# A Mamba and FFN layer on one core: dt products in pairs of row halves, the normalisation in four items, later stores, new order lists

## What is computed

```
xi, z = split(x @ W_in.T)                     # 512 + 512 channels
u  = silu(causal_conv4(xi) + conv_b)
dbl = u @ W_xproj.T                           # 16 (dt) + 16 (B) + 16 (C) columns
dt = softplus(dbl[:, :16] @ W_dt.T + b_dt)
h_t = h_(t-1) * exp(dt_t * A) + (dt_t * u_t) * B_t     # 512 channels x 16 states
y_t = sum_s h_t * C_t + u_t * D_skip
x1 = layernorm(x + (y * silu(z)) @ W_out.T)
out = layernorm(x1 + (silu(x1 @ wg.T) * (x1 @ wu.T)) @ wd.T)   # hidden width 768, int weights / 127
```

## Time and profile before

| | us |
|---|---|
| median of 3 runs | 1813.12 (1812.05 to 1816.79) |
| the profiled execution, its time | 1811.88 |
| its span, first to last instruction | 1810.2 |

### The profile page before, as it was taken

How to read it: one execution, slowest core, us unless ns; L and a number is a source line. 1 busy time by engine, 2 the same in 40 slices (tenths; PEclk the granted TensorE clock), 3 DMA queues, 4 the chain that set the end, 5 groups by cost and what they waited for, 6 DMA issues and landing times.

```text
span 1810.2 us, 40427 instructions
## 1 busy us (share of the span) xinstructions
PE 1738.4 (96%) x15678; PEld 1214.1 (67%) x15678; DVE 1708.0 (94%) x2003; ACT 1714.3 (95%) x2907; POOL 1496.8 (83%) x852
## 2 busy tenths in 40 slices
...
GB/s 209 1 119 1 23 98 15 118 1 114 19 15 118 14 118 1 59 74 15 117 10 123 1 15 118 15 118 1 90 43 15 118 12 120 1 54 67 1 25 24
DMA packets 171487, 100.57 MB, mean 56 GB/s; under 512 B 139408, under 2 KB 157584, under 8 KB 163232
## 3 DMA queue, kind: packets, MB, share of 16 engines
...
...
## 4 chain that ended last, share of the span: by engine, by line
PE 44%; ACT 28%; DVE 14%; issue 9%; POOL 4%; DMA 1%; SPq 0%; ACTq 0%; POOLq 0%; DVEq 0%
PE ring L1172 16%; PE tp L1151 13%; ACT decay L702 9%; ACT hT L709 8%; DVE h L913 7%; PE yb L1165 7%; PE ring L1264 4%; DVE acc L934 4%; POOL drive L568 3%; PE ring L1209 2%; ACT L739 2%; ACT acc L718 1%; ACT sz L739 1%; PE ring L1230 1%; ACT u L735 1%
## 5 line engine op out<-in xcount | busy, mean ns | idle before, releaser
L568 POOL TENSOR_TENSOR drive<-dtu,b_all 128x1024 f32<-128x1024 f32 x511 | 1217.1, 2417 | 9.7 <-DVE h L913 7.4
L702 ACT ACTIVATE decay<-dt,a_neg 128x512 f32<-128x512 f32 x1024 | 706.8, 718 | 9.5 <-DVE h L913 8.7
L1151 PEld LDWEIGHTS tp<-ident,h 128*128 128x128 f32 x4096 | 463.3, 141 | 251.4 <-issue 122.4
L913 DVE TENSOR_TENSOR_SCAN h<-decay,h,drive 128x512 f32<-128x512 f32 x512 | 620.8, 1268 | 8.7 <-ACT decay L702 4.5
L913 DVE TENSOR_TENSOR_SCAN h<-decay,drive 128x512 f32<-128x512 f32 x512 | 592.6, 1209 | 26.0 <-ACT decay L702 23.4
L709 ACT ACTIVATE hT<-tp 128x512 f32<-128x512 f32 x1024 | 596.8, 619 | 20.5 <-PE tp L1151 19.6
L1151 PE MATMUL tp<-ident,h 128*128 128x128 f32 x4096 | 564.2, 277 | 45.8 <-ACT hT L709 32.8
L1165 PE MATMUL yb<-hT,diag_c 128*32 128x128 f32 x8192 | 275.5, 277 | 6.5 <-ACT yt L730 5.3
L1165 PEld LDWEIGHTS yb<-hT,diag_c 128*32 128x32 f32 x8192 | 210.6, 110 | 82.0 <-issue 47.9
L1172 PE MATMUL ring<-xt,w_in 128*128 128x512 f32 x512 | 245.1, 602 | 2.4 <-ACT acc L750 2.4
L934 DVE SCALAR_TENSOR_TENSOR acc<-xi,cw,acc 128x512 f32<-128x512 f32 x189 | 160.0, 867 | 14.1 <-ACT xi L720 10.2
...
## 6 DMA issues: line engine op xcount, KB each, us to landing
b_all<-bc_scratch SPq DMA_DIRECT2D x63, 1024.0 KB, 6.9
xt<-in_xT SPq DMA_DIRECT2D x16, 512.0 KB, 4.4
res<-in_x SPq DMA_DIRECT2D x16, 512.0 KB, 5.8
out<-res SPq DMA_DIRECT2D x15, 512.0 KB, 2.9
c_col<-bc_scratch SPq DMA_DIRECT2D x256, 2.0 KB, 2.4
...
b_all<-bc_scratch SPq DMA_DIRECT2D x2, 512.0 KB, 4.6
...
```

The costliest lines, as they stand in the source:

```text
L568: tt(drive[:, j % 4, :, :], src, b_all[:, n:n + 2, :], ALU.mult).then_inc(g_dr, 1)
L702: act(decay[decay_slot(k.parity, i)][:, :], dt[:, cb, :], ACT.Exp, scale=a_neg[:, cb, n:n + 1]).then_inc(a_da, 1)
L913: nc.vector.tensor_tensor_scan(h[:, h_slot(k.parity, q), at:at + T, i % 4], decay[decay_slot(k.parity, i)][:, :], drive[:, (i // 2) % 4, i ...
L1151: last = nc.tensor.transpose(tp[g % 2][:, b * P:(b + 1) * P], h[:, h_slot(k.parity, q), t0:t0 + TS, :].rearrange("p t s -> p (t s)"), iden ...
```

## The change

**dt products.** w_dt gets a second copy of its 16 rows in rows 64 to 79, and from chunk 1 on a DMA on SP copies dbl's rows 0 to 15 into rows 64 to 79. In first and steady chunks dt 0 and 1, and dt 2 and 3, are issued as a pair, the first through rows 0 to 63, the second through rows 64 to 127, after a wait for both banks.
**Normalisation.** norm is four list items of one instruction each, with the same wait in each.
**Stores.** store(k-2) stands at the end of SP's chunk.
**Lists.** All lists are new. The core of the diff, with the steady lists in the places that the prediction speaks of:

```diff
 PE_SIDE = {
-    (0, 1): [("sum", 14)], (0, 3): [("z", 0)], (1, 1): [("sum", 15), ("z", 1), ("turn", 3)],
...
-    (5, 2): [("x1T", 0), ("sum", 3), ("x1T", 1)], (6, 0): [("gate", 0)], (6, 1): [("gate", 1)],
-    (6, 2): [("sum", 4)], (6, 3): [("up", 0), ("gate", 2), ("up", 1)], (7, 1): [("sum", 5), ("xproj", 0)],
-    (7, 3): [("gate", 3)], (8, 1): [("sum", 6), ("turn", 0)], (8, 3): [("gate", 4)], (9, 1): [("dt", 0)],
-    (9, 2): [("sum", 7)], (9, 3): [("gate", 5)], (10, 1): [("up", 2)], (10, 3): [("sum", 8)],
-    (11, 1): [("up", 3)], (11, 3): [("up", 4), ("sum", 9), ("sum", 10)], (12, 0): [("turn", 1)],
-    (12, 1): [("up", 5)], (12, 3): [("dt", 1), ("sum", 11)], (13, 1): [("down", 0), ("turn", 2)],
-    (13, 3): [("down", 1)], (14, 1): [("sum", 12)], (14, 3): [("dt", 2)], (15, 1): [("dt", 3)],
-    (15, 3): [("sum", 13)],
+    (0, 1): [("sum", 14)], (0, 3): [("xi", 0), ("sum", 15)], (1, 1): [("z", 0), ("turn", 3)],
...
+    (4, 1): [("x1T", 0), ("x1T", 1), ("sum", 2)], (4, 2): [("gate", 0)], (4, 3): [("gate", 1)],
+    (5, 0): [("up", 0), ("up", 1)], (5, 2): [("gate", 2)], (5, 3): [("sum", 3)], (6, 1): [("xproj", 0)],
+    (6, 3): [("sum", 4)], (7, 0): [("gate", 3)], (7, 2): [("gate", 4)], (7, 3): [("sum", 5)],
+    (8, 1): [("sum", 6)], (8, 3): [("up", 2)], (9, 1): [("turn", 0)], (9, 3): [("sum", 7)],
+    (10, 1): [("dt", 0), ("dt", 1)], (10, 2): [("sum", 8)], (10, 3): [("up", 3)], (11, 1): [("gate", 5)],
+    (11, 3): [("sum", 9)], (12, 0): [("sum", 10)], (12, 2): [("turn", 1)], (12, 3): [("up", 4)],
+    (13, 1): [("sum", 11)], (13, 3): [("up", 5), ("sum", 12), ("turn", 2)], (14, 1): [("down", 0)],
+    (14, 3): [("dt", 2), ("dt", 3)], (15, 1): [("down", 1)], (15, 3): [("sum", 13)],
 }
 ACT_SIDE = {
...
-    (3, 1): [("log", 1)], (3, 2): [("hT", 8), ("hT", 9)], (3, 3): [("xi", 1)], (4, 1): [("sz", 0), ("sz", 1)],
...
-    (6, 0): [("hT", 19), ("hT", 20), ("u", 0), ("hT", 21), ("u", 1), ("y", 0), ("tanh", 0), ("tanh", 1), ("u", 2), ("u", 3), ("hT", 22)],
-    (6, 3): [("tanh", 2), ("hT", 23), ("norm", 1)], (7, 0): [("hT", 24)], (7, 1): [("hT", 25)],
...
-    (11, 0): [("hT", 41)], (11, 1): [("hT", 42), ("hT", 43)], (11, 3): [("sz", 2)],
...
-    (13, 2): [("hT", 48)], (13, 3): [("sz", 3), ("hT", 49), ("log", 0)], (14, 2): [("hT", 50), ("hT", 51)],
...
+    (2, 1): [("hT", 5), ("z", 1)], (2, 2): [("hT", 6), ("z", 2)], (2, 3): [("hT", 7)], (3, 2): [("log", 1)],
+    (4, 0): [("sz", 0)], (4, 1): [("xi", 1), ("hT", 8), ("hT", 9)], (4, 3): [("hT", 10), ("xi", 2)],
+    (5, 0): [("hT", 11), ("xi", 3), ("hT", 12), ("z", 3), ("x1T", 0), ("x1T", 1), ("hT", 13), ("u", 0), ("hT", 14), ("u", 1), ("sz", 1), ("tanh", 0), ("u", 2), ("tanh", 1), ("hT", 15), ("u", 3)],
...
+    (10, 0): [("hT", 35), ("y", 1)], (10, 1): [("hT", 36)], (10, 2): [("hT", 37), ("bias", 0)],
+    (10, 3): [("hT", 38)], (11, 0): [("hT", 39), ("bias", 1)],
...
+    (13, 2): [("y", 2), ("hT", 50), ("hT", 51)], (14, 0): [("sz", 2), ("sz", 3), ("log", 0), ("hT", 52)],
+    (14, 1): [("hT", 53)], (14, 2): [("hT", 54), ("hT", 55), ("bias", 2)], (14, 3): [("hT", 56)],
+    (15, 1): [("hT", 57), ("norm", 1)], (15, 3): [("hT", 58), ("hT", 59), ("bias", 3)],
 }
 DVE_SIDE = {
-    (2, 1): [("skip", 3), ("clamp", 1)], (3, 3): [("conv", 0, 0), ("r1", 0)], (4, 2): [("r1", 1)],
-    (5, 3): [("max", 1), ("norm", 0), ("conv", 0, 1), ("conv", 1, 0), ("conv", 1, 1), ("conv", 2, 0), ("conv", 2, 1), ("conv", 3, 0), ("conv", 3, 1)],
-    (6, 0): [("gs", 0), ("gs", 1)], (6, 2): [("hid", 0)], (7, 0): [("gs", 2)], (7, 1): [("hid", 1)],
-    (8, 2): [("gs", 3), ("skip", 0)], (9, 2): [("gs", 4)], (10, 3): [("hid", 2), ("gs", 5)],
-    (11, 3): [("hid", 3), ("hid", 4)], (12, 1): [("skip", 1)], (12, 2): [("hid", 5)],
-    (14, 0): [("clamp", 0), ("r2", 0), ("skip", 2)], (14, 1): [("max", 0)], (15, 0): [("r2", 1)],
+    (1, 1): [("clamp", 1)], (1, 3): [("skip", 3)], (3, 2): [("r1", 0)], (4, 0): [("r1", 1)],
+    (4, 3): [("max", 1), ("conv", 0, 0), ("norm", 0, 0), ("norm", 0, 1), ("norm", 0, 2), ("norm", 0, 3), ("conv", 0, 1), ("conv", 1, 0), ("conv", 1, 1), ("conv", 2, 0), ("conv", 2, 1), ("conv", 3, 0), ("conv", 3, 1)],
+    (5, 0): [("gs", 0)], (5, 1): [("gs", 1)], (5, 2): [("hid", 0)], (6, 1): [("hid", 1)], (7, 1): [("gs", 2)],
+    (8, 1): [("gs", 3)], (8, 3): [("gs", 4)], (10, 0): [("skip", 0), ("hid", 2)], (11, 1): [("hid", 3)],
+    (12, 0): [("gs", 5)], (13, 1): [("skip", 1)], (13, 3): [("hid", 4), ("hid", 5), ("clamp", 0)],
+    (14, 0): [("skip", 2)], (14, 2): [("max", 0), ("r2", 0)], (15, 3): [("r2", 1)],
 }
...
 ACT_END = [
...
+    ("hT", 55), ("sz", 2), ("hT", 56), ("hT", 57), ("sz", 3), ("hT", 58), ("hT", 59), ("end_hT", 60), ("end_hT", 61),
...
 POOL_LAST = {
...
-    (4, 1): [("std", 0), ("diag", 3)], (7, 0): [("dtu", 1)], (11, 1): [("gate", 0)], (12, 1): [("gate", 1)],
-    (15, 0): [("gate", 2)],
...
+    (7, 0): [("dtu", 1)], (10, 1): [("gate", 0)],
 }
 POOL_END = [
-    ("end_std", 1),
+    ("gate", 1), ("gate", 2), ("end_std", 1),
 ]
...
             (w_dt[0:R, :], W_dtT),
+            (w_dt[P // 2:P // 2 + R, :], W_dtT),
...
             def spread_bc(k, with_b=False):
                 wait(eng, a_dbl, k.count(2, 2))
+                if k.index > 0:
+                    eng.dma_start(dbl[P // 2:P // 2 + R, :], dbl[0:R, :]).then_inc(st_two, 16)
                 eng.dma_start(bc_dram, dbl[R:R + 2 * N, :]).then_inc(st_bc, 16)
...
             def chunk(k, tail, head, more, late=True):
                 if tail:
                     load_res(k + -1)
-                if late:
-                    store(k + -2)
                 if head:
                     spread_bc(k + 1)
...
                         load_b(g)
+                if late:
+                    store(k + -2)
...
-            def normalise(k):
+            def normalise(k, blocks):
 
                 wait(eng, g_n[0], k.count(4, 4))
-                for tb in range(TB):
+                for tb in blocks:
...
-                if tail:
+                if what == "norm" and tail:
+                    normalise(k + -1, part)
+                elif tail:
                     rest_of_layer(k + -1, what, i)
...
+            def dt_pair(k, cb):
+
+                if cb == 0:
+                    eng.wait_ge(st_two, 16 * k.index)
+                room(place["dt", cb, k.index])
+                room(place["dt", cb + 1, k.index])
+                for i in range(2):
+                    rows = slice(i * P // 2, (i + 1) * P // 2)
+                    product(bank(k, "dt", cb + i)[:, :], [(w_dt[rows, (cb + i) * P:(cb + i + 1) * P], dbl[rows, :])], p_dt)
...
+                elif what == "dt" and kind != "last":
+                    if of[0] % 2 == 0:
+                        dt_pair(k + 1, of[0])
```

More of the change, by code:

```diff
@@ L96 @@
+    (15, 1): [("gate", 2), ("dtu", 0), ("diag", 0)],
 }
 PE_FIRST = {
-    (0, 3): [("xi", 0)], (1, 1): [("z", 0)], (1, 3): [("xi", 1)], (2, 2): [("z", 1)], (2, 3): [("xi", 2)],
-    (3, 0): [("sum", 0)], (3, 1): [("sum", 1)], (3, 3): [("sum", 2)], (4, 2): [("z", 2)], (5, 0): [("z", 3)],
-    (5, 2): [("sum", 3), ("xi", 3)], (7, 0): [("sum", 4)], (7, 1): [("sum", 5), ("xproj", 0)],
-    (8, 3): [("turn", 0), ("dt", 0), ("sum", 6)], (9, 1): [("sum", 7)], (9, 3): [("dt", 1)],
-    (10, 3): [("sum", 8)], (11, 1): [("sum", 9)], (11, 2): [("dt", 2)], (12, 0): [("turn", 1)],
@@ L105 @@
+    (12, 3): [("dt", 0), ("dt", 1), ("sum", 10), ("sum", 11), ("turn", 2)], (14, 0): [("sum", 12)],
+    (14, 3): [("dt", 2), ("dt", 3)], (15, 3): [("sum", 13)],
 }
 ACT_FIRST = {
[16 rows of a table removed]
[15 rows of a table added]
 }
 DVE_FIRST = {
-    (0, -1): [("clamp", 1)], (2, 2): [("max", 1)], (3, 2): [("conv", 0, 0)],
-    (7, 0): [("conv", 0, 1), ("conv", 1, 0), ("conv", 1, 1), ("conv", 2, 0), ("conv", 2, 1), ("conv", 3, 0), ("conv", 3, 1)],
-    (10, 0): [("skip", 0)], (12, 3): [("skip", 1)], (13, 0): [("clamp", 0)], (13, 3): [("max", 0)],
@@ L128 @@
-    (14, 2): [("skip", 2)],
+    (0, -1): [("clamp", 1)], (1, 0): [("conv", 0, 0)], (5, 3): [("conv", 0, 1), ("max", 1), ("conv", 1, 0)],
+    (6, 1): [("conv", 1, 1)], (9, 1): [("conv", 2, 0), ("conv", 2, 1), ("conv", 3, 0), ("conv", 3, 1)],
+    (9, 3): [("skip", 0)], (11, 0): [("skip", 1)], (13, 1): [("clamp", 0)], (13, 2): [("skip", 2)],
+    (14, 0): [("max", 0)],
 }
 POOL_FIRST = {
-    (3, 0): [("first_diag", 0), ("first_diag", 1)], (3, 1): [("first_diag", 2)], (5, 1): [("first_diag", 3)],
@@ L137 @@
-    (2, 0): [("turn", 3)], (2, 1): [("sum", 0)], (2, 3): [("out", 0)], (3, 1): [("out", 1)],
-    (3, 3): [("sum", 1)], (4, 0): [("z", 3)], (4, 3): [("sum", 2), ("sum", 3)],
-    (5, 0): [("x1T", 0), ("x1T", 1)], (5, 2): [("gate", 0)], (5, 3): [("gate", 1)], (6, 0): [("gate", 2)],
-    (6, 2): [("up", 0)], (6, 3): [("up", 1), ("turn", 0), ("sum", 4), ("sum", 5)], (7, 1): [("up", 2)],
-    (7, 3): [("gate", 3)], (8, 1): [("sum", 6)], (8, 3): [("gate", 4)], (9, 0): [("up", 3)],
```

(25 more changed lines are left out.)

49 lines of the change are left out of this document (25 added, 24 removed), and 82 rows, old and new, of tables (ACT_FIRST, ACT_LAST, ACT_SIDE).

## The result

The changed kernel takes 1874.18 us (median of 4 runs, 1871.68 to 1874.88); the kernel before took 1812.59 beside it. The ratio is 1.0336, 95% interval [1.0318, 1.0354]: **61.6 us slower**, where 18.6 faster was forecast, far outside the range.

What follows compares the result with a forecast made beforehand. Even chunks were taken as bound by ACT and PE, odd by DVE. Seven pairs at 2.3 us (-16), with +0.6 -2 -3 +1.7, took 1811.9 to 1793; plus 1.2 for the median, 1794.5, range 1785 to 1810.

Steps and rivals of the forecast that it cites:

- The change takes nothing off DVE: DVE's work stays, so two chunks cannot fall below 212.95 us from 216.05; at most 3.1 us per pair.
- nine short ones, 0.67 each: DVE's gs, hid, skip and clamp instructions from skip 0 to r2 0, counted at 6 us of 28.
- 6 us of cover: Slack from DVE having 37 us to skip 0 where PE has 31 to turn 0; meant to absorb the bank waits.
- Bank waits costed at nothing: Each dt pair on PE waits for two free ring banks; this was put at nothing on DVE's path.
- rival B: PE stands at pair two for a scan, max 0 and r2 0's add, 2.2 us per chunk: 1831; chance 0.08.
- PE -0.70 per chunk: Pairs save PE 1.14 us per chunk, extra detours return 0.44; two chunks fall from 213.78 to 212.4.
- D: Row halves do not run beside each other on PE, adding 0.58 and 0.43 us per chunk: 1824; chance 0.04.
- Odd chunks by DVE: DVE, busy 106.96 of 108.13 us, was read as what bounds odd chunks.
- even chunks are bound by ACT and PE: Of an even chunk's 107.92 us ACT is busy 107.53 and PE 106.49, so these were read as its bound.
- The burst: DVE's convolutions move behind scan 19 with one more tap, about 11 us with max 1 and norm.
- What would show it: Signs set beforehand; wrong if odd chunks exceed 108.5 us, PE stands before w_dt for DVE, or w_dt steps stay 0.43.
- case C: PE stands about 0.7 us per chunk for pair two's second bank, leaving time unchanged at 1811; chance 0.10.

Runs made afterwards that it cites:

- e6: The changed kernel with the clamp in a one-port form that also reduces into a spare column: 1813.88 us, 1.0016 of the kernel before.
- e7: The changed kernel with r2 0 ahead of max 0 on DVE in the steady chunks, old clamp kept: 1870.04 us, 1.0326 of the kernel before.
- e11: The changed kernel with single dt products instead of pairs and the one-port clamp: 1822.27 us, 1.0059 of the kernel before.
- e12: e6 with five tile detours joined in PE's steady list: 1873.58 us, 1.0343 of the kernel before.
- e14: e6 with two detours joined in PE's steady list, sum 8 behind dt 0 and 1, sum 10 beside sum 9: 1818.58 us.
- e8: The kernel before with sz 2 moved beside sz 3 on ACT in steady chunks, meant to save two table loads per chunk: 1818.2 us, 1.0041.
- e4: The kernel before with only the store moved to the end of SP's chunk: 1809.7 us, 0.9998.
- e1: The changed kernel with heads on POOL moved from (5, 0) to (6, 1) in the steady list: 1903.37 us, 1.0518 of the kernel before.

## Why the prediction was wrong

- **"The change takes nothing off DVE", floor 212.95 per two chunks: the step that failed.** It is true of the work and false of the time: the wait for GpSimd inside the clamp was put at nothing, without a reason. I carried the clamp at 0.67 us through a change of all lists; it took 4.1, 14 times, and 2.7, 6 times, which is 14 x 3.4 + 6 x 2.05 = 60 us. e6 gets 59 us back. Of these 42 are DVE's time in the clamps, whose new form is no longer blocked but slower by itself; the rest is what followed from them. The "nine short ones, 0.67 each" of the count from skip 0 to r2 0 hold the same clamp: 3.4 of the 6 us of cover went there. The cue stood in the trace before, in the group of the taps and in the timeline shown above:

```profile
L934 DVE SCALAR_TENSOR_TENSOR acc<-xi,cw,acc 128x512 f32<-128x512 f32 x189 | 160.0, 867 | 14.1 <-ACT xi L720 10.2
```

A mean of 867 ns where most taps take 0.75 us, and a clamp of 0.97 at 554.23 beside a drive of 2.81 instead of 2.38. A group whose mean lies above its shortest instruction has a second price, set by what runs beside it, and no list of counts shows it.
- **Bank waits costed at nothing, and rival B.** The wait came, and as B described it: 1.5 us per chunk ahead of pair two, through scan, max 0 and r2 0. But its cause was the clamp in front, not PE's earliness; without the blocking it is gone (e6), and taking it away alone gives 3 us (e7). B had the sign and the place, and not the mechanism: 1831 for it, 1874 measured. The fallen clock behind it was in no rival.
- **PE -0.70 per chunk.** The pairs' own term was right: -1.14 per chunk forecast, and e6 against e11 has 2.4 us less of PE per two chunks. The four w_dt instructions of a pair take 1.13 us from first start to last end, 4.5 us busy in two chunks (e6) instead of 7.6 (e11) and 8.2 (before); D falls. The term that was too small is what the lists give back: 0.44 per chunk forecast, 1.2 measured (e11 has 216.2 us per two chunks, the kernel before 213.8). So PE has the same 213.8 us in e6 as before (213.78), not 212.4. The transposes, the same 4096, take 580.6 us instead of 564.2. I took that for the price of more detours; e12 and e14 joined detours and PE's busy time did not fall (215.0 and 213.9 per two chunks), so why the transposes are slower stays open.
- **"Odd chunks by DVE".** The rows did not say so: in the odd chunk PE was busy for 107.29 us and DVE for 106.96. With PE at 213.8 the floor of two chunks is 213.8 and not 212.95, so that without any blocking at most 2.3 us per pair, not 3.1, were there to win.
- **ACT.** The 94 loads came, and 210.7 us per two chunks for the 209.3 forecast. The reading "even chunks are bound by ACT and PE" fell on its first half: in e8 the even chunks have 2.5 us less of ACT and are 0.4 us longer. PE is the busiest engine in both kernels, 213.8 of 216.05 and of 216.5 us per two chunks, with DVE close behind, and I take its order for the bound; that is argued, not shown, since of 2.4 us more of PE in e11 only 1.1 came out in the time. In either case -5.1 us of ACT had little to win.
- **Small steps.** Norm in four items: nothing more was seen (argued, not tried alone). Store and SP: nothing (e4). The burst: covered, and better than thought, 16 us less in the taps; that GpSimd stands in heads beside it fits e1, where it does not and they take 173.1. Head +0.7 for +0.6; behind the last scan +2.7 for +1.7; last chunk -4.6 for -3; chunk 0 +2.0 for -2.
- **"What would show it"** named the right signs: odd chunks over 108.5 (113.9), PE standing ahead of w_dt. Without the blocking the time is that of case C, next to no difference (e6, +0.16%), to which I gave 0.10. But that is C's number and not its mechanism: C needed 0.7 us of standing per chunk for the pair's second bank, and in e6 PE has no such wait; its busy time did not fall instead.
